# Attention in batches of three units, and attention and scan programs written out without loops

## The chip, the cores and the metric

The kernel runs on one core of a Trainium2 chip. A core has a matrix engine (TensorE, PE in the profile), a vector engine (VectorE, DVE), a scalar engine (ScalarE, ACT), GpSimd (POOL) and SyncE (SP), which issues transfers. Each runs its own program in order, and they meet at semaphores. Matmul results go to PSUM (eight banks of 2 KB per partition); everything else is in SBUF. The metric is the device time of one execution in microseconds.

## The reference, cut to what matters

The input is an image of 48 channels and 128 x 128 pixels. Four layers are applied, each as x = x + f(group_norm(x)). The change touches two of them.

Layer 0 is attention over all 16,384 pixels, one head of 48 channels:

```python
qkv = conv3x3_depthwise(einsum(x, qkv_w)); q, k, v = split(qkv)
q, k = l2norm(q), l2norm(k)
attn = softmax(q @ k.T * temperature)        # 16384 x 16384
out = (attn @ v) @ proj_w.T
```

Layer 2 is a state-space scan over 4,096 tokens of 192 channels, cut here to the rows that matter:

```python
h = exp(d_l[:, None] * A) * h + (d_l * u_l)[:, None] * B_l[None, :]   # 192 x 192 state
y = einsum('dn,n->d', h, C_l)
```

Layer 1 (an 8 x 8 FFT mixing with gates) and layer 3 (integral-image sampling) are not touched.

## The kernel before

**Attention** (`attend`, line 467). The queries are cut into 32 blocks of 512 (`NQB`, `BLK`), and for each block the keys are cut into 64 units (`UNITS`): a unit is 2 x 128 keys against 512 queries, so there are 2,048 units. For each unit:

- PE `score` (line 532): six f16 matmuls, on two halves of 64 rows of the array at a time, into one of two slots of `scores` (two PSUM banks a slot). It waits until ACT has read the slot.
- ACT `exponentials` (line 600): one Exp of 128 x 1024 into one of four slots of `prob` (`RING`).
- DVE `low` (line 633): the difference between the f32 probability and its upper half read as bf16, kept as f16 in `prob_lo`.
- PE `weigh_high` (line 547): four matmuls of the values against the upper halves, on two halves of 64 columns of the array; `weigh_low` (line 559): two matmuls against `prob_lo`. Both add to one of two banks of `sums`. `weigh_low` ends the use of the slot (`used`).

PE's order is written by hand in `pair_of_blocks` (line 574): for every two units it runs `weigh_high` and `weigh_low` of the two units that lie four back (`AHEAD`), then `score` of two new ones. Twice per pair of blocks, `project` (line 568) multiplies the finished sums, which ACT copied to SBUF (`copy_sums`, line 607), with the output weights into the bank `final`; DVE then inverts and multiplies in eight pieces (`invert`, `divide`), spread over the units 16 to 47 of the next block, and POOL adds the block to the image (line 525), once per block.

PE's body is a pair of blocks, written out, and a loop runs it 15 times after a first copy. ACT's and DVE's programs are nested loops: four units are the innermost body, and a block or a pair is the outer one. SP loads a block of queries one block ahead.

**Scan** (`scan`, line 1244). 192 channels are taken in 32 groups of six (`NG`, `GD`). A group has 36 steps (`STEPS`: nine slots of 128 state rows, four chunks of 1,024 tokens). In each step PE spreads delta and delta times u over the partitions (`delta`, `delta_u`: two matmuls each), ACT copies one and takes Exp of the other, POOL multiplies the copy by B (line 1527), and DVE runs one scan of 128 x 1024 (line 1487). Beside this PE computes y of the chunk before (`unit`, `select`), and DVE cuts the diagonal out of it (`extract`, line 1498), four times per nine steps. The state changes between two buffers; in PE's, ACT's, DVE's and POOL's programs the group is the body of a loop. PE and ACT run group 0 as a copy, groups 1 to 30 in the loop and group 31 as a copy; DVE and POOL run groups 1 to 31 in the loop.

Waits whose value comes from a loop register are followed by `nop(nofuse=True)`, an instruction that does nothing; without it the wait can ride on the next instruction.

Of the kernel before, what the change touches and what calls it, by code (L numbers as in the profile page):

```python
# [204 lines left out]
PAIR = 2 * UNITS  # L205
# [4 lines left out]
RING = 4  # L210
PIECES = 8
AHEAD = 4
# [254 lines left out]
def attend(nc, image, halves, values, out_w, bound, temp):  # L467


    with ExitStack() as ctx:  # L470
# [16 lines left out]
        ngroup = UNITS // RING  # L487
        q_hi, q_lo = halves[0, LO, :], halves[1, LO, :]
        k_hi, k_lo = halves[0, HI, :], halves[1, HI, :]
        tops, tails = [slice(r * CHUNK, r * CHUNK + C) for r in range(2)], [slice(r * CHUNK + C, (r + 1) * CHUNK) for r in range(2)]  # L490

# [37 lines left out]
        def _(pe):  # L529
            def score(pair, u, first):  # L530
                slot, g = u // UNITS, u % UNITS
                if g == 0:
                    pe.wait_ge(q_loaded[slot], 128 * (pair + 1))
                if first and slot == 0 and g % (UNITS // KPIECES) == 0:
                    pe.wait_ge(k_loaded[g // (UNITS // KPIECES)], 128)
                if not first or u > 1:
                    pe.wait_ge(prob_ready, pair * PAIR + u - 1)
                pe.nop(nofuse=True)
                for j in range(3):
                    for r in range(2):  # L540
                        part = slice(r * CHUNK, (r + 1) * CHUNK)
                        last = nc.tensor.matmul(scores[:, u % 2, r * BLK:(r + 1) * BLK], keys[part, j, g * KT:(g + 1) * KT],  # L542
                                                queries[part, slot, j, :], start=j == 0, stop=j == 2)
                last.then_inc(scores_ready, 1)

            def weigh_high(pair, u, first=False):
                slot, g = (u // UNITS) % 2, u % UNITS
                if g == 0 and not first:
                    pe.wait_ge(sums_copied, pair * 2 + u // UNITS - 1)
                pe.wait_ge(prob_ready, pair * PAIR + u + 1)  # L550
                pe.nop(nofuse=True)
# [6 lines left out]
            def weigh_low(pair, u):  # L558
                slot, g = (u // UNITS) % 2, u % UNITS
                pe.wait_ge(low_ready, pair * PAIR + u + 1)  # L560
                pe.nop(nofuse=True)
# [5 lines left out]
            def project(b, first=False):  # L567
                pe.wait_ge(sums_copied, b + 1)
                if not first:
                    pe.wait_ge(divided, b * PIECES)  # L570
                pe.nop(nofuse=True)
                nc.tensor.matmul(final[:, :], out_w[:, :], sums_sb[:, :], start=True, stop=True).then_inc(projected, 1)

            def pair_of_blocks(pair, first=False):
                for u in range(0, PAIR, 2):
                    if not first or u >= AHEAD:
                        for v in (u - AHEAD, u - AHEAD + 1):
                            weigh_high(pair, v, first)
                        for v in (u - AHEAD, u - AHEAD + 1):
                            weigh_low(pair, v)  # L580
                    if u == 12 and not first:
                        project(pair * 2 - 1)
                    if u == UNITS + 12:
                        project(pair * 2, first)
                    score(pair, u, first)
                    score(pair, u + 1, first)

            pair_of_blocks(0, first=True)
            with pe.Fori(1, NQB // 2) as pair:
                pair_of_blocks(pair)  # L590
            for u in range(PAIR - AHEAD, PAIR, 2):
                for v in (u, u + 1):
                    weigh_high(NQB // 2 - 1, v)
                for v in (u, u + 1):
                    weigh_low(NQB // 2 - 1, v)
            project(NQB - 1)

        @block.scalar
        def _(act):
            def exponentials(s, j, wait_used=True):  # L600
                act.wait_ge(scores_ready, s + 1)
                if wait_used:
                    act.wait_ge(used, s + 1 - RING)
                nc.scalar.activation(prob[:, j, :], scores[:, j % 2, :], ACT.Exp, bias=bound[:, 0:1],  # L604
                                     scale=temp[:, 0:1]).then_inc(prob_ready, 1)

            def copy_sums(b, slot, first=False):
                act.wait_ge(used, (b + 1) * UNITS)
                if not first:
                    act.wait_ge(projected, b)  # L610
                act.nop(nofuse=True)
                nc.scalar.copy(sums_sb[:, :], sums[:, slot, :]).then_inc(sums_copied, 1)

            def query_block(b, slot, first=False, second=False):
                s0 = b * UNITS
                for j in range(RING):
                    exponentials(s0 + j, j, wait_used=not first)
                for j in range(RING):
                    exponentials(s0 + RING + j, j)
                    if j == 0 and not first:  # L620
                        copy_sums(b - 1, 1 - slot, first=second)
                with act.Fori(2, ngroup) as g:
                    for j in range(RING):
                        exponentials(s0 + g * RING + j, j)
            query_block(0, 0, first=True)
            query_block(1, 1, second=True)
            with act.Fori(1, NQB // 2) as pair:
                for slot in range(2):
                    query_block(pair * 2 + slot, slot)
            copy_sums(NQB - 1, 1)  # L630

        @block.vector
        def _(dve):
            def low(s, j, wait_used=True):
                dve.wait_ge(prob_ready, s + 1)
                if wait_used:
                    dve.wait_ge(used, s + 1 - RING)
                nc.vector.tensor_tensor(prob_lo[:, j, :], prob[:, j, :], prob_hi[:, j, :],  # L638
                                        ALU.subtract).then_inc(low_ready, 1)

            def invert(b, piece, first=False):
                dve.wait_ge(projected, b + 1)
                if not first:
                    dve.wait_ge(added, b)
                dve.nop(nofuse=True)
                q = ds(piece * (BLK // PIECES), BLK // PIECES)
                nc.vector.reciprocal(rden[HI, q], final[LO, q]).then_inc(inverted, 1)

            def divide(b, piece):
                dve.wait_ge(inverted, b * PIECES + piece + 1)  # L650
                dve.nop(nofuse=True)
                q = ds(piece * (BLK // PIECES), BLK // PIECES)
                nc.vector.tensor_tensor(rden[HI, q], final[HI, q], rden[HI, q], ALU.mult).then_inc(divided, 1)  # L653

            def query_block(b, first=False, second=False):
                s0 = b * UNITS
                for j in range(RING):
                    low(s0 + j, j, wait_used=not first)

                def groups(g0, g1, divides=False):  # L660
                    with dve.Fori(g0, g1) as g:
# [14 lines left out]
            with dve.Fori(2, NQB) as b:  # L676
                query_block(b)
# [1499 lines left out]
```

## Time and profile before

| | |
|---|---|
| median of 3 runs | 8340.8 us (8329.88 to 8345.57) |
| the profiled execution | 8343.99 us |
| its span, first to last instruction | 8339.0 us |
| outside the span | 5.0 us |
| PE, DVE, ACT, POOL busy | 80%, 84%, 63%, 40% of the span |
| Exp of attention, first to last start | 426.2 to 3479.6 us |
| first scan step | 4424.6 us |
| Exp in attention (line 604) | 2,048 times, 1202 ns each |
| scans (line 1487) | 1,152 times, 2280 to 2348 ns each |

Busy time of PE is modelled at its end: a matmul is shown with the time in which its result runs out of the array, and the next one starts before that. The distance from one start to the next is what counts. "Issue" behind a wait means that nothing in the profile released the instruction: its engine's sequencer had not handed it over, or the array was not ready. PEclk is the share of the full TensorE clock that was granted.

### The profile page before, as it was taken

How to read it: one execution, taken by the hardware profiler on the slowest of the kernel's cores; microseconds unless marked ns; L12 is line 12 of the kernel's file. 1: busy time of each engine (PE TensorE's matmuls, PEld its weight loads, DVE VectorE, ACT ScalarE, POOL GpSimd, SP SyncE). 2: the span in 40 equal slices, each digit the busy share in tenths (PEclk: the TensorE clock that was granted, in tenths of full speed). 3: DMA queues.
4: the chain of work that ended last, by engine and by line, in shares of the span. 5: the costliest groups of instructions: out<-in, count | busy, mean ns of one | idle time of the engine just before them, and what ended most of it. 6: DMA issues, size and time to landing. Idle time of an engine off the chain costs nothing. (4 is left out here: it accounts for less than half of the span.)

```text
span 8339.0 us, 181301 instructions
## 1 busy us (share of the span) xinstructions
PE 6705.5 (80%) x61152; PEld 2911.9 (35%) x61152; DVE 6983.8 (84%) x6264; ACT 5257.7 (63%) x5277; POOL 3359.4 (40%) x1726
## 2 busy tenths in 40 slices
PE   4999999999999999799697788788878878834321
PEld 2533333333333333255332333333333333322110
DVE  7788888888888888788748999999999999964556
ACT  2177777777777777522187888888888888820000
POOL 1000000000000000000007999999999999934666
PEclk9999999999999999899899999999999999967665
DMA  1020000000000000000020000000000000022222
GB/s 27 26 38 5 5 5 5 7 5 5 5 5 5 7 5 5 4 0 0 12 60 15 6 6 6 6 6 6 6 6 6 6 7 6 6 56 74 67 66 74
DMA packets 116941, 139.45 MB, mean 17 GB/s; under 512 B 49884, under 2 KB 96060, under 8 KB 115148
## 3 DMA queue, kind: packets, MB, share of 16 engines
q1 hardware_dynamic: 91488, 76.06, 3.7%
q0 software_dynamic: 24576, 50.36, 2.3%
q8 instruction: 585, 9.58, 0.5%
q10 hardware_dynamic: 256, 3.15, 0.3%
q14 instruction: 36, 0.29, 0.0%
HBM read 93.83 MB, written 35.65 MB: 16 GB/s over the span
## 5 line engine op out<-in xcount | busy, mean ns | idle before, releaser
L1527 POOL TENSOR_TENSOR k_image<-k_image,s_b 128x1024 f32<-128x1024 f32 x1152 | 2697.0, 2354 | 457.9 <-ACT k_image L1437 421.0
L604 ACT ACTIVATE att_prob<-att_scores,a_bound,a_temp 128x1024 f32<-128x1024 f32 x2048 | 2361.4, 1202 | 692.5 <-PE att_scores L542 689.7
L638 DVE TENSOR_TENSOR att_prob_lo<-att_prob 128x1024 f16<-128x1024 f32 x2048 | 2451.1, 1238 | 410.1 <-ACT att_prob L604 365.7
L542 PE MATMUL att_scores<-att_queries,att_keys 64*128 64x512 f16 x12288 | 1520.6, 380 | 22.7 <-DMA att_keys<-qk_halves 19.2
L1437 ACT COPY k_image<-h_du 128x1024 f32<-128x1024 f32 x1152 | 1169.3, 1015 | 434.4 <-PE h_du L1366 433.2
L525 POOL TENSOR_TENSOR k_image<-k_image,att_rden 48x512 f32 x32 | 69.1, 2159 | 3334.2 <-DVE att_rden L653 3334.2
L1487 DVE TENSOR_TENSOR_SCAN h_state_odd<-h_keep,k_image 128x1024 f32<-128x1024 f32 x576 | 1327.1, 2348 | 0.1
L1444 ACT ACTIVATE h_keep<-h_keep,h_decay 128x1024 f32<-128x1024 f32 x1152 | 1258.8, 1093 | 65.2 <-PE h_keep L1354 44.2
L555 PE MATMUL att_sums<-att_prob,a_values 128*64 128x512 bf16 x8192 | 1136.1, 398 | 42.8 <-issue 42.8
L1354 PE MATMUL h_keep<-h_rows,h_spread 128*128 128x512 bf16 x2304 | 703.0, 387 | 466.2 <-DVE k_image L1487 217.9
L542 PEld LDWEIGHTS att_scores<-att_queries,att_keys 64*128 64x128 f16 x12288 | 540.6, 94 | 928.8 <-issue 627.0
L1366 PE MATMUL h_du<-h_rows,h_spread 128*128 128x512 bf16 x2304 | 714.7, 393 | 126.4 <-issue 98.6
L1487 DVE TENSOR_TENSOR_SCAN k_image<-h_keep,k_image 128x1024 f32<-128x1024 f32 x288 | 648.1, 2280 | 87.4 <-ACT h_keep L1444 79.6
L1487 DVE TENSOR_TENSOR_SCAN k_image<-h_keep,h_state_odd,k_image 128x1024 f32<-128x1024 f32 x288 | 663.5, 2348 | 0.0
L1714 POOL DMA_INDIRECT b_shared<-cells,b_index x512 | 496.0, 969 | 342.9 <-issue 148.6
L563 PE MATMUL att_sums<-att_prob_lo,a_values 128*64 128x512 f16 x4096 | 623.2, 381 | 8.9 <-DVE att_prob_lo L638 8.9
L555 PEld LDWEIGHTS att_sums<-att_prob,a_values 128*64 128x64 f16 x8192 | 372.9, 108 | 715.7 <-issue 483.9
L1354 PEld LDWEIGHTS h_keep<-h_rows,h_spread 128*128 128x128 bf16 x2304 | 157.4, 98 | 997.5 <-issue 988.1
L1764 PE MATMUL b_ps_t<-k_ident,b_mean 128*48 128x128 f32 x128 | 33.5, 417 | 573.3 <-DVE b_mean L1880 373.6
L1797 ACT ACTIVATE b_act<-b_ps_c,b_b,b_back 112x512 f32<-112x512 f32 x32 | 24.9, 777 | 643.4 <-remote 358.1
L563 PEld LDWEIGHTS att_sums<-att_prob_lo,a_values 128*64 128x64 f16 x4096 | 233.1, 110 | 265.0 <-issue 28.5
L1385 PE MATMUL h_y<-h_state_odd,s_c 128*32 128x192 f32 x4096 | 321.2, 350 | 1.8 <-DVE h_state_odd L1487 1.8
(275 smaller groups left out, 7293.3 us busy)
## 6 DMA issues: line engine op xcount, KB each, us to landing
y_rows<-h_y_sb SPq DMA_DIRECT2D x1024, 3.0 KB
att_queries<-qk_halves SPq DMA_DIRECT2D x256, 48.0 KB, 2.0
parts<-t_part SPq DMA_DIRECT2D x48, 192.0 KB, 2.5
h_rows<-parts SPq DMA_DIRECT2D x128, 72.0 KB
b_shared<-cells,b_index POOLq DMA_INDIRECT x512
att_keys<-qk_halves SPq DMA_DIRECT2D x64, 96.0 KB, 7.2
cells<-b_shared SPq DMA_DIRECT2D x4, 1536.0 KB, 5.1
qk_halves<-qkv_hi SPq DMA_DIRECT2D x32, 112.0 KB, 1.8
```

The lines of the kernel that those rows point to most:

```text
L542: last = nc.tensor.matmul(scores[:, u % 2, r * BLK:(r + 1) * BLK], keys[part, j, g * KT:(g + 1) * KT], queries[part, slot, j, :], start=j ...
L555: nc.tensor.matmul(sums[part, slot, :], values[:, r * UNITS + g, part], prob_hi[:, u % RING, r * BLK:(r + 1) * BLK], start=g == 0 and r == ...
L563: last = nc.tensor.matmul(sums[r * CHUNK:(r + 1) * CHUNK, slot, :], values[:, r * UNITS + g, 0:CHUNK], prob_lo[:, u % RING, r * BLK:(r + 1 ...
L604: nc.scalar.activation(prob[:, j, :], scores[:, j % 2, :], ACT.Exp, bias=bound[:, 0:1], scale=temp[:, 0:1]).then_inc(prob_ready, 1)
L638: nc.vector.tensor_tensor(prob_lo[:, j, :], prob[:, j, :], prob_hi[:, j, :], ALU.subtract).then_inc(low_ready, 1)
L1354: last = nc.tensor.matmul(keep[:, k % 2, cols], spread[:, 0, slot, :], rows[:, c % 2, cols], start=True, stop=True)
L1366: last = nc.tensor.matmul(du[:, cols], spread[:, 1, slot, :], rows[:, c % 2, cols], start=True, stop=True)
L1437: nc.scalar.copy(du_sb[k % 3], du[:, :]).then_inc(du_copied, 1)
L1444: nc.scalar.activation(keep[:, k % 2, :], keep[:, k % 2, :], ACT.Exp, scale=decay[:, ds(g * SLOTS + k // STEPS * SLOTS + k % SLOTS, 1)]).t ...
L1487: nc.vector.tensor_tensor_scan(out=state[c % 2][:, slot, :], data0=keep[:, k % 2, :], data1=drive[k % 3], initial=initial, op0=ALU.mult, o ...
L1527: nc.gpsimd.tensor_tensor(drive[k % 3], du_sb[k % 3], b[:, c * CH:(c + 1) * CH], ALU.mult).then_inc(drive_ready, 1)
L1714: nc.gpsimd.indirect_dma_start(got[:, y % GOT, k * CELL:(k + 1) * CELL], None, cells, bass.IndirectOffsetOnAxis(index[:, k, y:y + 1], 0)). ...
```

## The change

- Attention works in batches of three units (`BATCH`): three slots of `scores` (six banks), a ring of six in `prob` and `prob_lo`, and weighing six units back. A batch is `weigh_high` of three, `weigh_low` of three, `score` of three. Batches run on over the ends of blocks.
- The bank `final` goes: `project` writes its result into the bank of `sums` that it was computed from, and the first `weigh_high` of a block waits for `divided` of the block two back instead of for `sums_copied`.
- `project` comes after the weighing of unit 12 of the next block, `copy_sums` after the Exp of unit 6, and `invert` and `divide` run in the units 18 to 49.
- All loops of the two stages on PE, ACT, DVE and POOL are written out, apart from POOL's loop over blocks in attention. SP's loops stay. Waits have constant values, and the `nop(nofuse=True)` are gone.

```diff
+BATCH = 3
-RING = 4
+RING = 2 * BATCH
-AHEAD = 4
+AHEAD = 2 * BATCH
+PROJECT_AT = 12
+INVERT_FROM = 18
...
-        scores = n.ps("scores", [P, 2, 2 * BLK])
+        scores = n.ps("scores", [P, BATCH, 2 * BLK])
-        final = n.ps("final", [SPAN, BLK])
...
+            def score(u):
+                b, g, slot = u // UNITS, u % UNITS, u // UNITS % 2
...
+                wait_past(pe, prob_ready, u + 1 - BATCH)
...
+            def weigh_high(u):
+                if g == 0:
+                    wait_past(pe, divided, (b - 1) * PIECES)
+                pe.wait_ge(prob_ready, u + 1)
...
+            def project(b):
                 pe.wait_ge(sums_copied, b + 1)
+                nc.tensor.matmul(sums[0:SPAN, b % 2, :], out_w[:, :], sums_sb[:, :], start=True, stop=True).then_inc(projected, 1)
+
+            for u0 in range(0, ALL_UNITS + AHEAD, BATCH):
+                weighed = [u for u in range(u0 - AHEAD, u0 - AHEAD + BATCH) if 0 <= u < ALL_UNITS]
+                for u in weighed:
+                    weigh_high(u)
+                for u in weighed:
+                    weigh_low(u)
+                for u in weighed:
+                    if u >= UNITS and u % UNITS == PROJECT_AT:
+                        project(u // UNITS - 1)
+                for u in range(u0, u0 + BATCH):
+                    if u < ALL_UNITS:
+                        score(u)
...
+            for u in range(ALL_UNITS):
+                act.wait_ge(scores_ready, u + 1)
+                wait_past(act, used, u + 1 - RING)
+                nc.scalar.activation(prob[:, u % RING, :], scores[:, u % BATCH, :], ACT.Exp, bias=bound[:, 0:1],
                                      scale=temp[:, 0:1]).then_inc(prob_ready, 1)
+                if u >= UNITS and u % UNITS == RING:
+                    copy_sums(u // UNITS - 1)
...
+            for u in range(ALL_UNITS):
+                low(u)
+                b, g = u // UNITS, u % UNITS
+                if b and g >= INVERT_FROM and g < INVERT_FROM + 4 * PIECES:
+                    piece, step = divmod(g - INVERT_FROM, 4)
+                    if step == 0:
+                        invert(b - 1, piece)
+                    if step == 2:
+                        divide(b - 1, piece)
...
             delta(0, 0)
             delta_u(0, 1)
-            group(0, first=True)
-            with pe.Fori(1, NG - 1) as g:
-                group(g)
-            group(NG - 1, last=True)
+            for g in range(NG):
+                group(g, first=g == 0, last=g == NG - 1)
```

The last edit stands in the same form in ACT's, DVE's and POOL's scan programs.

## Rows read from the trace of the kernel before

**Rows 1.** Two windows (attention, scan): busy us of PE, PEld, DVE, ACT, POOL; clock, DMA.

```profile
424.00:3484.00 3060.00, 3003.28 (x24639) 1155.27 (x24640) 2644.34 (x2544) 2373.22 (x2080) 67.83 (x31) 0.99 0.03 7
4424.00:7324.00 2900.00, 2326.48 (x31018) 1006.64 (x31018) 2807.67 (x1660) 2406.17 (x2556) 2695.16 (x1152) 0.98 0.02 6
```

**Rows 2.** Timeline of attention: start us, length us, engine, line, operation, count [idle before].

```profile
2001.12 1.47 PE L542 MATMUL att_scores<-att_queries,att_keys 64*128 64x512 f16 x12
2002.06 2.30 ACT L604 ACTIVATE att_prob<-att_scores,a_bound,a_temp 128x1024 f32<-128x1024 f32 x2 [0.57 <-PE att_scores L542]
2002.52 1.10 PE L555 MATMUL att_sums<-att_prob,a_values 128*64 128x512 bf16 x8
2003.46 0.60 PE L563 MATMUL att_sums<-att_prob_lo,a_values 128*64 128x512 f16 x4
2003.99 1.25 PE L542 MATMUL att_scores<-att_queries,att_keys 64*128 64x512 f16 x10
```

**Rows 3.** The same timeline from inside two of these runs of matmuls.

```profile
2002.99 0.63 PE L555 MATMUL att_sums<-att_prob,a_values 128*64 128x512 bf16 x4
...
2003.67 0.38 PE L563 MATMUL att_sums<-att_prob_lo,a_values 128*64 128x512 f16 x2
```

**Rows 4.** Timeline of POOL in attention: one addition per query block.

```profile
590.05 2.15 POOL L525 TENSOR_TENSOR k_image<-k_image,att_rden 48x512 f32 x1 [499.33 <-DVE att_rden L653]
683.49 2.17 POOL L525 TENSOR_TENSOR k_image<-k_image,att_rden 48x512 f32 x1 [91.28 <-DVE att_rden L653]
...
873.68 2.19 POOL L525 TENSOR_TENSOR k_image<-k_image,att_rden 48x512 f32 x1 [94.56 <-DVE att_rden L653]
...
3459.49 2.19 POOL L525 TENSOR_TENSOR k_image<-k_image,att_rden 48x512 f32 x1 [91.27 <-DVE att_rden L653]
```

**Rows 5.** Timeline of PE at the end of a pair of blocks.

```profile
989.52 1.86 PE L555 MATMUL att_sums<-att_prob,a_values 128*64 128x512 bf16 x8 [2.85 <-issue]
```

**Rows 6.** Busy time by engine in the stretch behind that.

```profile
989.60:993.00 3.40, 3.40 (x17) 1.24 (x17) 0.24 (x1) 0.00 (x0) 0.00 (x0) 0.50 0.30 81
```

**Rows 7.** Timeline of PE at a projection and at unit 50.

```profile
1010.01 1.11 PE L572 MATMUL att_final<-att_sums_sb,a_out_w 128*112 128x512 f32 x2
1011.06 1.47 PE L542 MATMUL att_scores<-att_queries,att_keys 64*128 64x512 f16 x12
...
1068.49 0.41 PE L563 MATMUL att_sums<-att_prob_lo,a_values 128*64 128x512 f16 x2 [0.27 <-DVE att_prob_lo L638]
```

**Rows 8.** Timeline of DVE while it inverts and divides.

```profile
1033.48 2.36 DVE L638 TENSOR_TENSOR att_prob_lo<-att_prob 128x1024 f16<-128x1024 f32 x2
1035.87 0.23 DVE L653 TENSOR_TENSOR att_rden<-att_final,att_rden  x1
...
1038.63 0.55 DVE L647 RECIPROCAL att_rden<-att_final  x1
1039.21 2.36 DVE L638 TENSOR_TENSOR att_prob_lo<-att_prob 128x1024 f16<-128x1024 f32 x2
```

**Rows 9.** Timeline of DVE at the first steps of scan groups 1, 2 and 31.

```profile
4513.00 4.51 DVE L1487 TENSOR_TENSOR_SCAN k_image<-h_keep,k_image 128x1024 f32<-128x1024 f32 x2
...
4600.62 2.29 DVE L1487 TENSOR_TENSOR_SCAN k_image<-h_keep,k_image 128x1024 f32<-128x1024 f32 x1
4606.07 2.29 DVE L1487 TENSOR_TENSOR_SCAN k_image<-h_keep,k_image 128x1024 f32<-128x1024 f32 x1 [3.16 <-ACT h_keep L1444]
...
7236.50 4.47 DVE L1487 TENSOR_TENSOR_SCAN k_image<-h_keep,k_image 128x1024 f32<-128x1024 f32 x2
```

**Rows 10.** Timeline of PE at the start of scan group 2.

```profile
4602.84 1.01 PE L1366 MATMUL h_du<-h_rows,h_spread 128*128 128x512 bf16 x2 [3.70 <-issue]
```

**Rows 11.** Timeline of PE in the convolution ahead of attention.

```profile
220.69 1.89 PE L191 MATMUL qkv_ps_qk<-qkv_x_split,qkv_qk_split 112*112 x8
222.42 1.02 PE L409 MATMUL qkv_ps_n<-qkv_sq,qkv_ones 112*112 112x512 f32 x2
```

**Rows 12.** The DMA queues in attention: packets, MB, share of 16 engines.

```profile
q8 instruction: 251, 4.11, 0.6%
```

More of the change, by code:

```diff
@@ L204 @@
 UNITS = KHALF // KT
-PAIR = 2 * UNITS
+ALL_UNITS = NQB * UNITS
+BATCH = 3
 CHUNK = 64
@@ L529, in _ @@
         def _(pe):
-            def score(pair, u, first):
-                slot, g = u // UNITS, u % UNITS
+            def score(u):
+                b, g, slot = u // UNITS, u % UNITS, u // UNITS % 2
                 if g == 0:
[L533 to L538, printed above, removed]
+                    pe.wait_ge(q_loaded[slot], 128 * (b // 2 + 1))
+                if b == 0 and g % piece_units == 0:
+                    pe.wait_ge(k_loaded[g // piece_units], 128)
+                wait_past(pe, prob_ready, u + 1 - BATCH)
                 for j in range(3):
@@ L541, in score @@
                         part = slice(r * CHUNK, (r + 1) * CHUNK)
-                        last = nc.tensor.matmul(scores[:, u % 2, r * BLK:(r + 1) * BLK], keys[part, j, g * KT:(g + 1) * KT],
+                        last = nc.tensor.matmul(scores[:, u % BATCH, r * BLK:(r + 1) * BLK], keys[part, j, g * KT:(g + 1) * KT],
                                                 queries[part, slot, j, :], start=j == 0, stop=j == 2)
                 last.then_inc(scores_ready, 1)
[L546 to L551, printed above, removed]
+            def weigh_high(u):
+                b, g, slot = u // UNITS, u % UNITS, u // UNITS % 2
+                if g == 0:
+                    wait_past(pe, divided, (b - 1) * PIECES)
+                pe.wait_ge(prob_ready, u + 1)
                 for r in range(2):
@@ L599, in _ @@
         def _(act):
[L600 to L604, printed above, removed]
-                                     scale=temp[:, 0:1]).then_inc(prob_ready, 1)
[L607 to L630, printed above, removed]
+            def copy_sums(b):
+                act.wait_ge(used, (b + 1) * UNITS)
+                wait_past(act, projected, b)
+                nc.scalar.copy(sums_sb[:, :], sums[:, b % 2, :]).then_inc(sums_copied, 1)
+            for u in range(ALL_UNITS):
+                act.wait_ge(scores_ready, u + 1)
+                wait_past(act, used, u + 1 - RING)
+                nc.scalar.activation(prob[:, u % RING, :], scores[:, u % BATCH, :], ACT.Exp, bias=bound[:, 0:1],
+                                     scale=temp[:, 0:1]).then_inc(prob_ready, 1)
+                if u >= UNITS and u % UNITS == RING:
+                    copy_sums(u // UNITS - 1)
@@ L649, in divide @@
             def divide(b, piece):
                 dve.wait_ge(inverted, b * PIECES + piece + 1)
-                dve.nop(nofuse=True)
                 q = ds(piece * (BLK // PIECES), BLK // PIECES)
[L653 to L661, printed above, removed]
-                        for j in range(RING):
-                            low(s0 + g * RING + j, j)
-                            if divides and j == 1:
-                                invert(b - 1, g - g0, second)
-                        if divides:
-                            divide(b - 1, g - g0)
-                if first:
-                    groups(1, ngroup)
-                else:
-                    groups(1, 4)
-                    groups(4, 4 + PIECES, divides=True)
-                    groups(4 + PIECES, ngroup)
@@ L674, in _ @@
-            query_block(0, first=True)
-            query_block(1, second=True)
-            with dve.Fori(2, NQB) as b:
-                query_block(b)
+                nc.vector.tensor_tensor(rden[HI, q], sums[HI, b % 2, q], rden[HI, q], ALU.mult).then_inc(divided, 1)
+            for u in range(ALL_UNITS):
[7 more added lines that the diff above has]
+                        divide(b - 1, piece)
@@ L1468, in _ @@
             copy_du(0, 1)
-            group(0, first=True)
-            with act.Fori(1, NG - 1) as g:
-                group(g)
-            group(NG - 1, last=True)
+            for g in range(NG):
+                group(g, first=g == 0, last=g == NG - 1)
             for half in range(2):
@@ L1511, in group @@
                     recur(g, k)
-            group(0, first=True)
-            with dve.Fori(1, NG) as g:
-                group(g)
+            for g in range(NG):
+                group(g, first=g == 0)
             for slot in range(SLOTS):
@@ L1524, in group @@
                     wait_past(pool, state_ready, s - 2)
-                    pool.nop(nofuse=True)
                     b = b_c[0 if slot < GD else 1]
@@ L1528, in group @@
                                             ALU.mult).then_inc(drive_ready, 1)
-            group(0)
-            with pool.Fori(1, NG) as g:
+            for g in range(NG):
                 group(g)
```

62 lines of the change are left out of this document (12 added, 50 removed).

## The prediction

> **What bounds the kernel now.** I read the busy time by engine in the two changed stages first. In attention PE is busy 3003 of 3060 us, DVE 2644, ACT 2373; in the scan DVE is busy 2808 of 2900 us, POOL 2695, PE 2326 [rows 1]. So PE should set the pace of attention and DVE that of the scan. The timelines then show what the share can't.
>
> In attention one turn of PE's program takes 2003.99 - 2001.12 = 2.87 us for two units, 1.435 us a unit [rows 2], and PE stands in front of no wait: score, weigh_high, weigh_low and the next score follow each other. But they don't follow at an even pace. Matmuls come in pairs that share the array. The twelve of a score pair of units take 1.47 us from the first start to the last end, and one takes 0.38 us [rows 2, 3], so six pairs start within 1.09 us, 0.218 us apart. From the last of them (2002.21) to the first weigh_high (2002.52) it is 0.31 us. Inside weigh_high the distance is (2003.46 - 2002.99) / 2 = 0.235 us, in weigh_low 2003.67 - 2003.46 = 0.21 us, and from the last weigh_low to the next score 2003.99 - 2003.67 = 0.32 us [rows 2, 3]. So twice per turn, where the array goes from halves of rows to halves of columns and back, some 0.1 us is lost. The turn from weigh_high to weigh_low, which also has waits, loses nothing. ACT is not the limit: it has 0.57 us idle per turn [rows 2].
>
> The timeline of POOL gives the length of each block, as it adds one block each. It has 31 additions. From 590.05 to 683.49 is 93.44 us, but 873.68 comes 2.19 + 94.56 = 96.7 us after the one before, and this longer distance returns at every second block [rows 4]. There PE issues nothing for 2.85 us [rows 5] and then runs at a granted clock of 0.50, which is the 1.2 GHz level, for 3.4 us [rows 6]. It is the point where PE's loop over pairs jumps back. In the scan the same thing stands at each group: group 1, which PE and ACT reach from the copy of group 0 without a jump, takes 4600.62 - 4513.00 = 87.62 us; at the start of group 2 PE issues nothing for 3.70 us [rows 10], and the second scan waits 3.16 us for ACT's Exp [rows 9]. From group 2 to group 31 the 29 groups take 7236.50 - 4600.62 = 2635.88 us, 90.89 each [rows 9]. Group 31 starts with two scans back to back (4.47 us for two), though DVE and POOL jump there as well; PE and ACT don't. So the jumps of DVE and POOL cost nothing that shows.
>
> **The change part by part.** The sum is made against the profiled execution: 8344.0 us, of which 8339.0 are span. The median is 3.2 us less.
>
> *Three units per turn.* A turn now has a third unit: three more score pairs (3 x 0.218 = 0.65), two of weigh_high (2 x 0.235 = 0.47) and one of weigh_low (0.21), 1.33 us, and no further change of the array's halves. Turn: 2.87 + 1.33 = 4.20 us, 1.400 a unit, 0.035 less than now; x 2,048 = 72 us. The bounds: nothing, if what is lost belongs to the unit and not to the turn; 98 us, if every one of the six added pairs comes at 0.215 us (turn 4.16). I take 72, since the distances were read at the very places that multiply.
>
> A page weighs this otherwise. The Trainium skill (TensorEngine Tiling (Array Packing), Key Properties) says that a change of tiling mode drains the engine. With a full drain the next matmul would start when the last is out, 0.38 us after its start, 0.16 more than a pair's distance; two of those are 0.32 us per turn, and the saving would be 0.32 x (1/2 - 1/3) x 2,048 = 109 us. The rows show 0.31 and 0.32 us, so a partial drain.
>
> *Does anything else keep up with 4.20 us?* ACT: two Exps take 2.30 us [rows 2], three 3.45; 0.75 us are free, and copy_sums (about half an Exp's elements, some 0.6 us) fits once per block. The third score needs the third Exp of the turn before. An Exp starts 0.94 us after its score's first matmul (2002.06 - 2001.12), so the three of a turn end at 0.94 + 3.45 = 4.39 us, and the third score of the next turn starts at 4.20 + 1.31 = 5.51: 1.1 us to spare, and copy_sums takes 0.6 of it. The ring of six holds: weigh_low of six units back ends ahead of the score, and the Exp comes later still. DVE: while it inverts and divides, four units take 1039.21 - 1033.48 = 5.73 us, of which 2 x 2.36 + 0.23 + 0.55 = 5.50 are busy [rows 8]. PE will want 5.60. If 5.73 is DVE's own limit, it falls 0.13 us behind in each of eight pieces, 1.0 us per block. DVE finishes the low of a turn's third unit near 0.94 + 3.45 + 1.3 = 5.7 us after the turn's first score, and weigh_low of it comes at about 4.20 + 1.96 + 1.41 + 0.42 = 8.0: 2.3 us of cover. So nothing; 31 x 1.0 = 32 us without that cover.
>
> *project* keeps its price: 1011.06 - 1010.01 = 1.05 us of PE per block [rows 7]. That it writes into `sums` makes the block after next wait for `divided`, which is complete at unit 50 of the next block; that wait is never late.
>
> *The jumps in attention.* 3459.49 - 590.05 = 2869.4 us are 30 blocks; at 93.45 they would be 2803.5. The loop costs 66 us (14 jumps within this, 4.7 us each, idle PE and the low clock behind it together) [rows 4 to 6]. Written out, all of it goes. What is late next is PE itself.
>
> *The inner loops of ACT and DVE.* A straight block has 32 turns (91.8) and project (1.05); 93.45 - 92.85 = 0.6 us are left. One piece is the wait of weigh_low for DVE at unit 50, where DVE goes from one of its loops to the next [rows 7]; another is copy_sums. With straight programs and the deeper ring I take all: 31 x 0.6 = 19 us. Bounds 0 and 19.
>
> *The scan.* 29 x (90.89 - 87.62) = 95 us [rows 9]. DVE is then without a gap, and its pace is measured in group 1 and stays. POOL has 2695 / 1,152 = 2.34 us per step [rows 1] against 87.62 / 36 = 2.43, so it follows, with little to spare. At least the 3.16 us wait of rows 9 less what DVE had in hand goes; I see no reason for a part of it to stay.
>
> *The nops.* Without them a wait can ride on the next instruction. DVE's and ACT's attention instructions had none before. On PE the place to look is the convolution: its second instruction group (line 409) carries its wait without a nop, and starts 222.42 - (220.69 + 1.89 - 0.38) = 0.22 us after the last matmul, the ordinary distance [rows 11]. Nothing either way.
>
> *Filling the programs.* PE's attention is the same number of matmuls, read once. The instruction queue brought 251 blocks in attention, 0.6% of the DMA engines [rows 12], and PE ran through most of them in straight stretches of two blocks without a loss. Nothing for the fetch of longer programs.
>
> Sum: 72 + 66 + 19 + 95 = 252 us. Profiled execution 8092, median 8340.8 - 252 = 8089 us.
>
> **The rivals.**
> *DVE becomes the bound of attention while it divides.* For it: 5.73 us against 5.60. Against it: 5.73 is also exactly twice PE's turn, so DVE may only follow, and there is cover. It gives back 32 us: 8121.
> *The loss belongs to the unit, not to the turn.* Then batches of three bring nothing: 8161. Against it: the loss stands at the two changes of halves alone.
> *The full drain.* By the matmul's own length the two changes would cost 0.32 us per turn: 109 instead of 72 us, 8052. The page named above would have it so; the rows speak for less.
> *Slower: waits on PE's weight loads expose them.* In a turn of three there are nine waits, seven of which are not at a change of halves. If a wait that rides on a weight load keeps it from being loaded under the running matmuls, each costs what a change does, 0.1 us: 7 x 683 turns x 0.1 = 478 us, 8567. It decides from 252 / 4,781 = 0.053 us a wait. For it: each of these loads was ahead of time only because the nop took the wait. Against it: rows 11, though with the whole array and not halves.
> *Slower or less: the fetch of straight programs.* ACT and DVE had short bodies in attention and now run through some 6,000 instructions each, 24 blocks of 256. If each new block stopped the engine as a jump does, 2.85 us, attention would lose 137 us and the scan more, some 70 blocks. It decides from 252 / 118 = 2.1 us a block. Against it: PE meets far more blocks and shows the loss at jumps only. The Trainium skill (Runtime: NRT & Kernel Launch, Instruction fetch mechanics) states just this: fetch ahead is sequential, and a taken branch out of the window stops it; by that rule, too, nothing stays, and the trace agrees with its even 93.45 us.
>
> **How the numbers follow.** Forecast 0.70, DVE bound 0.10, no gain from the turn 0.06, full drain 0.06, weight loads 0.05, fetch 0.03. The forecast's own spread is the 98 against 72 us on one side (8063) and the 19 us of the inner loops on the other (8108). To leave out no more than 2 in 10, the range reaches to the full drain below and the no-gain case above: 8048 to 8165. This program can be told from no change by 0.2%, 17 us. Faster needs one of the first four, or a small price in the last two: 0.92. Within 0.2%: 0.02. Slower: 0.06.
>
> **What would show it.** POOL's additions evenly 4.20 x 64 / 3 + 1.05 = 90.6 us apart, with no longer distance at every second one, shows turns, inner loops and jumps right at once; 92.5 would be the loss in the unit. A turn's timeline should hold 18, 12 and 6 matmuls in 4.20 us. All scan groups should be 87.6 us, and the granted clock 1.00 throughout both stages. PE idle for DVE's low at the units 18 to 49 would be the first rival; weight loads that start with their matmuls inside a run of equal ones, the slower one. Most of all the prediction would be wrong if the stall at PE's jump returned somewhere in the straight program.

## The result

The changed kernel takes 8076.3 us (median of 4 runs, 8070.6 to 8077.7) against 8342.5 us of the kernel before (4 runs beside it). The ratio is 0.9682, 95% interval 0.967 to 0.9695. The forecast was 8089 us, so the gain is 266 us where 252 were expected. The profiled execution's span is 8075.4 us instead of 8339.0.

The busy time by engine in the two stages of the changed kernel, as in [rows 1]:

```profile
425.00:3320.00 2895.00, 2883.49 (x24636) 1180.49 (x24630) 2635.80 (x2563) 2334.74 (x2081) 65.91 (x32) 1.00 0.03 7
4253.00:7056.00 2803.00, 2206.78 (x30510) 976.23 (x31018) 2801.54 (x1660) 2411.65 (x2556) 2698.89 (x1152) 1.00 0.02 6
```

PE in attention and DVE in the scan now have next to no idle time, and the granted clock is 1.00 in both. From the first Exp of attention to the last it is 3304.4 - 425.1 = 2879.3 us (3053.4 before), from the first scan to the last 7053.8 - 4253.5 = 2800.4 us (2897.2 before). These are 174 and 97 us less. Some 7 us were lost elsewhere, in code that wasn't changed: the stretch between attention and scan takes 949.1 instead of 945.0 us, the one behind the scan 1021.5 instead of 1017.2, and what is ahead of attention 1 us less. Why isn't shown. The first of these stretches lies anywhere from 943.7 (low_first) to 951.6 us (two_visits) in the experiments below, none of which touches it.

POOL's timeline in attention, one addition per query block, against [rows 4]:

```profile
585.18 2.06 POOL L527 TENSOR_TENSOR k_image<-k_image,att_rden 48x512 f32 x1 [495.75 <-DVE att_rden L616]
675.28 2.07 POOL L527 TENSOR_TENSOR k_image<-k_image,att_rden 48x512 f32 x1 [88.04 <-DVE att_rden L616]
765.41 2.08 POOL L527 TENSOR_TENSOR k_image<-k_image,att_rden 48x512 f32 x1 [88.07 <-DVE att_rden L616]
855.37 2.10 POOL L527 TENSOR_TENSOR k_image<-k_image,att_rden 48x512 f32 x1 [87.87 <-DVE att_rden L616]
...
3287.35 2.10 POOL L527 TENSOR_TENSOR k_image<-k_image,att_rden 48x512 f32 x1 [87.88 <-DVE att_rden L616]
```

The distances are 90.10, 90.13 and 89.96 us and repeat so to the end, (3287.35 - 585.18) / 30 = 90.07 on the mean. No second block is longer any more. The repeat over three blocks is the turn of three against 64 units.

PE's timeline in attention, against [rows 2, 3, 7]:

```profile
1701.99 2.12 PE L542 MATMUL att_scores<-att_queries,att_keys 64*128 64x512 f16 x18
1704.04 1.55 PE L554 MATMUL att_sums<-att_prob,a_values 128*64 128x512 bf16 x12
1705.42 0.81 PE L561 MATMUL att_sums<-att_prob_lo,a_values 128*64 128x512 f16 x6
1706.16 1.11 PE L567 MATMUL att_sums<-att_sums_sb,a_out_w 128*112 128x512 f32 x2
1707.21 2.12 PE L542 MATMUL att_scores<-att_queries,att_keys 64*128 64x512 f16 x18
```

A turn holds 18, 12 and 6 matmuls and takes 2.05 + 1.38 + 0.74 = 4.17 us (forecast 4.20); the mean of the 451 turns without a projection between 1,200 and 3,200 us is 4.173. The projection still costs 1.05 us. 64 / 3 turns of 4.173 us and 1.05 us are 90.07 us: nothing is left over in a block.

ACT's and DVE's timelines show how much is in hand:

```profile
1693.62 0.59 ACT L588 COPY att_sums_sb<-att_sums 128x512 f32<-128x512 f32 x1
1694.51 3.40 ACT L593 ACTIVATE att_prob<-att_scores,a_bound,a_temp 128x1024 f32<-128x1024 f32 x3 [0.30 <-PE att_scores L542]
1698.68 3.40 ACT L593 ACTIVATE att_prob<-att_scores,a_bound,a_temp 128x1024 f32<-128x1024 f32 x3 [0.78 <-PE att_scores L542]
```

```profile
1029.74 2.36 DVE L604 TENSOR_TENSOR att_prob_lo<-att_prob 128x1024 f16<-128x1024 f32 x2
1032.13 0.55 DVE L611 RECIPROCAL att_rden<-att_sums 48x64 f32<-48x64 f32 x1
1032.71 2.36 DVE L604 TENSOR_TENSOR att_prob_lo<-att_prob 128x1024 f16<-128x1024 f32 x2
1035.11 0.23 DVE L616 TENSOR_TENSOR att_rden<-att_sums,att_rden 48x64 f32<-48x64 f32 x1
1035.37 5.71 DVE L604 TENSOR_TENSOR att_prob_lo<-att_prob 128x1024 f16<-128x1024 f32 x4
```

ACT waits 0.78 us per turn for scores, and the copy of the sums fits into one such wait and leaves 0.30 us. On DVE a low now starts 0.26 us after the start of a divide. In the kernel before it was 1036.24 - 1035.87 = 0.37 us:

```profile
1034.91 2.30 ACT L604 ACTIVATE att_prob<-att_scores,a_bound,a_temp 128x1024 f32<-128x1024 f32 x2 [0.57 <-PE att_scores L542]
1036.24 2.36 DVE L638 TENSOR_TENSOR att_prob_lo<-att_prob 128x1024 f16<-128x1024 f32 x2
```

The first of these Exps, 1.20 us long, ends at 1036.11, and the low that reads it starts 0.13 us later, so it waited for the Exp and not for the divide. DVE had been following ACT there, and ACT in turn PE. DVE's own limit was 5.73 - 0.11 = 5.62 us for four units, about what the rows above show (1035.37 - 1029.74).

In the scan, DVE's timeline at the starts of groups 2 and 31, against [rows 9]:

```profile
4428.09 4.44 DVE L1424 TENSOR_TENSOR_SCAN k_image<-h_keep,k_image 128x1024 f32<-128x1024 f32 x2
...
6968.50 2.26 DVE L1424 TENSOR_TENSOR_SCAN k_image<-h_keep,k_image 128x1024 f32<-128x1024 f32 x1
```

These 29 groups take (6968.50 - 4428.09) / 29 = 87.60 us each, the 87.62 us that group 1 took before.

### The profile page after: what moved, and what is told of

It reads as the page before. It is cut to its first block and busy times, and to the rows that moved or that the text cites. A ratio compares the mean times of both kernels' runs of the same rounds, so it can differ in the third digit from the quotient of the medians.

```text
span 8075.4 us, 153634 instructions
## 1 busy us (share of the span) xinstructions
PE 6464.9 (80%) x60643; PEld 2907.0 (36%) x61152; DVE 6964.3 (86%) x6264; ACT 5223.3 (65%) x5277; POOL 3370.7 (42%) x1726
## 5 line engine op out<-in xcount | busy, mean ns | idle before, releaser
L593 ACT ACTIVATE att_prob<-att_scores,a_bound,a_temp 128x1024 f32<-128x1024 f32 x2048 | 2320.5, 1201 | 558.2 <-PE att_scores L542 558.0
L542 PE MATMUL att_scores<-att_queries,att_keys 64*128 64x512 f16 x12288 | 1447.3, 378 | 19.3 <-DMA att_keys<-qk_halves 19.3
L554 PE MATMUL att_sums<-att_prob,a_values 128*64 128x512 bf16 x8192 | 1056.5, 391 | 0.0
L1313 PE MATMUL h_du<-h_rows,h_spread 128*128 128x512 bf16 x1796 | 585.6, 385 | 105.0 <-issue 80.4
L554 PEld LDWEIGHTS att_sums<-att_prob,a_values 128*64 128x64 f16 x8192 | 400.6, 108 | 602.0 <-issue 288.9
L561 PE MATMUL att_sums<-att_prob_lo,a_values 128*64 128x512 f16 x4096 | 554.1, 378 | 0.0
L1302 PEld LDWEIGHTS h_keep<-h_rows,h_spread 128*128 128x128 bf16 x2304 | 133.1, 97 | 1076.5 <-DVE h_state_odd L1424 489.3
L1331 PE MATMUL h_y<-k_image,s_c 128*32 128x192 f32 x4096 | 324.0, 336 | 0.0
```

The lines of the kernel that those rows point to most:

```text
L542: last = nc.tensor.matmul(scores[:, u % BATCH, r * BLK:(r + 1) * BLK], keys[part, j, g * KT:(g + 1) * KT], queries[part, slot, j, :], star ...
L554: nc.tensor.matmul(sums[part, slot, :], values[:, r * UNITS + g, part], prob_hi[:, u % RING, r * BLK:(r + 1) * BLK], start=g == 0 and r == ...
L561: last = nc.tensor.matmul(sums[r * CHUNK:(r + 1) * CHUNK, slot, :], values[:, r * UNITS + g, 0:CHUNK], prob_lo[:, u % RING, r * BLK:(r + 1 ...
L593: nc.scalar.activation(prob[:, u % RING, :], scores[:, u % BATCH, :], ACT.Exp, bias=bound[:, 0:1], scale=temp[:, 0:1]).then_inc(prob_ready, 1)
L1302: last = nc.tensor.matmul(keep[:, k % 2, cols], spread[:, 0, slot, :], rows[:, c % 2, cols], start=True, stop=True)
L1313: last = nc.tensor.matmul(du[:, cols], spread[:, 1, slot, :], rows[:, c % 2, cols], start=True, stop=True)
```

## The experiments

The expectations give totals as on the chip of the first comparison. The chips of the experiments run the kernel before in 8218 to 8222 us and the changed kernel in 7952 us (after_again, 0.9676): what lies behind the scan takes 894 us there instead of 1021, with attention and scan alike. So the ratios are against the kernel before on the same chip, and the changed kernel is compared by its blocks and groups, whose lengths are the same on both. Where a total is said to lie above the changed kernel's, it is against the 7952.1 us of after_again, beside which only low_first and dense_pieces ran; the others ran on other chips.

**Batches of two, all else straight (b2_straight).**

```diff
-BATCH = 3
+BATCH = 2
```

> The changed kernel with batches of two (two score slots, ring of four, weighing four units back), all programs still without loops. My theory: a turn costs 2.87 us as in the kernel before, and the straight programs of ACT and DVE alone remove the 0.6 us that each block had left over, so POOL's additions stand 32 x 2.87 + 1.05 = 92.9 us apart and the attention stage takes (1.435 - 4.173 / 3) x 2048 = 90 us longer than in the changed kernel: 8166 us. Rival one: the loss belongs to the unit and not to the turn (then the batch brings nothing and this kernel takes 8076 us). Rival two: the 0.6 us went because the ring became deeper; then the blocks stay at 93.45 us and the kernel takes 8185 us.

It takes 8047.0 us, ratio 0.9789 (0.9773 to 0.9805), some 95 us above the changed kernel. POOL's timeline in attention:

```profile
684.20 2.07 POOL L527 TENSOR_TENSOR k_image<-k_image,att_rden 48x512 f32 x1 [90.93 <-DVE att_rden L616]
...
3381.46 2.09 POOL L527 TENSOR_TENSOR k_image<-k_image,att_rden 48x512 f32 x1 [90.93 <-DVE att_rden L616]
```

29 blocks take 2697.26 us, 93.01 each, and none is longer. So batches of three are worth 93.01 - 90.07 = 2.94 us a block. A turn of two takes 2.867 us in the traces of this kernel and of the kernel before, so 32 turns and a projection are 92.79 us. A straight block of the kernel before had 93.45 - 92.79 = 0.66 us left over, of which 0.44 are gone here and 0.22 stay; the turn itself accounts for 2.72 of the 2.94 us. Rival one (loss per unit) falls. Rival two (the ring did it) falls for two thirds of what was left over.

Where the 0.44 us went, the two traces show turn by turn: some 0.37 us near unit 50, where DVE went from one of its loops to the next, and 0.09 at copy_sums. That it was the loops of ACT and DVE alone isn't shown: this kernel also projects into `sums`, inverts and divides one unit later and has no nops.

**PE's loop back in the scan (scan_pe_loop), and its counterpart (scan_others_loop).**

```diff
-            for g in range(NG):
-                group(g, first=g == 0, last=g == NG - 1)
+            group(0, first=True)
+            with pe.Fori(1, NG - 1) as g:
+                group(g)
+            group(NG - 1, last=True)
```

The first has this on PE, with the nops; the second has the old loops and nops on ACT, DVE and POOL.

> The changed kernel with PE's program of the scan as it was before (loop over groups 1 to 30, with its nops); ACT, DVE and POOL stay without loops. My theory: the stall at a group's start is PE's jump alone, so groups take 90.9 us again and the kernel 8076 + 29 x 3.3 = 8172 us, with PE at the clock level 0.50 for a few us at each group. Rival: ACT's jump is as much to blame, as ACT's loop had the same bounds; then this kernel loses only part of it, down to nothing (8076 us) if it was ACT's alone.

> The counterpart: the changed kernel with the scan programs of ACT, DVE and POOL as they were before (loops and nops), PE's without a loop. My theory: jumps of these three cost nothing that shows, so groups take 87.6 us and the kernel 8076 us, within 8. Rival (ACT's jump is to blame): groups of about 90.9 us, 8172 us. If both this kernel and the one with PE's loop are slow, any jump costs.

PE's loop: 8046.0 us, ratio 0.9786 (0.9769 to 0.9802), 94 us slower than the changed kernel, groups of 90.90 us. The others' loops: 7956.1 us, ratio 0.9676 (0.966 to 0.9692), no slower, groups of 87.58 us. DVE's timeline at group 2, first with PE's loop, then with the others':

```profile
4427.57 2.29 DVE L1430 TENSOR_TENSOR_SCAN k_image<-h_keep,k_image 128x1024 f32<-128x1024 f32 x1
4432.95 2.29 DVE L1430 TENSOR_TENSOR_SCAN k_image<-h_keep,k_image 128x1024 f32<-128x1024 f32 x1 [3.09 <-ACT h_keep L1391]
```

```profile
4430.88 4.47 DVE L1430 TENSOR_TENSOR_SCAN k_image<-h_keep,k_image 128x1024 f32<-128x1024 f32 x2
```

PE's timeline at the same place, and its clock in the window behind it, both with PE's loop:

```profile
4429.79 1.01 PE L1315 MATMUL h_du<-h_rows,h_spread 128*128 128x512 bf16 x2 [3.70 <-issue]
```

```profile
4428.20:4434.00 5.80, 3.87 (x30) 1.76 (x32) 2.71 (x2) 2.01 (x2) 2.14 (x2) 0.52 0.08 17
```

DVE names ACT's Exp as what it waited for, and ACT's own loop is straight here. The stall of 3.70 us is that of [rows 10], at the same group. It is PE's alone.

The trace also records the branch itself, at the end of PE's loops (ns, least, median and most of all passes). First the kernel before, its loop over pairs of blocks and its loop over groups, then scan_pe_loop:

```profile
L589 PEldq COMPARE_BRANCH  x15: 76/3578/3898, 795.6 to 3478.2; - x15
L1423 PEldq COMPARE_BRANCH  x30: 83/3527/3851, 4598.7 to 7234.6; - x30
L1372 PEldq COMPARE_BRANCH  x30: 83/3552/3884, 4425.7 to 7061.7; - x30
```

The last pass of each loop, which doesn't jump back, is the one of 76 or 83 ns; the jumps take 3.3 to 3.9 us. In attention they take as long as in the scan.

**How long may PE's body be (pe_loop_short, pe_loop_mid, pe_loop_most).** All three have PE's loop and leave out part of y: the second and third matmul group of each unit, in four, two or one of a group's four chunks.

```diff
-                for stat, d0, d1, s0 in ((2, 0, GD, 0), (3, 0, half_d, GD), (4, half_d, GD, GD)):
+                for stat, d0, d1, s0 in ((2, 0, GD, 0), (3, 0, half_d, GD), (4, half_d, GD, GD))[:3 if c in (0, 2) else 1]:
```

(This is the middle one; the short one has `()`, the long one `(0, 2, 3)`. The nops are back with the loop. Each was run twice.)

> The changed kernel with PE's loop in the scan, and a shorter body: the two smaller of the three matmul groups of each unit are left out in all four chunks (part of y is not computed), so one group has some 1,110 instructions on PE by the profile's count, where the loop before has 2,130. DVE's work is the same. My theory: a jump stalls PE only where the body is longer than what the instruction memory holds, since PE's loops of 380 and 579 instructions in other stages show no gap; so groups take 87.6 us and PE's clock stays at 1.00 at their start. Rival: a jump always costs some 4 us and the other loops hide it behind waits; then groups take about 90.9 us.

> The same with the two smaller matmul groups left out in two chunks of four: some 1,620 instructions in PE's body. If the size decides, this tells on which side of it the limit lies: groups of 87.6 us (it still fits) or of about 90.9 us (it doesn't). By the Trainium skill (Runtime: NRT & Kernel Launch, Instruction fetch mechanics), PE's instruction memory holds 2,048, and it should fit.

> The same with the two smaller matmul groups left out in one chunk of four: some 1,870 instructions in PE's body. It should still fit by 2,048, unless the blocks of 256 at its two ends are counted whole: 1,870 instructions can touch nine blocks, eight are held. So 87.6 us a group, or a stall as with the full body; I hold these for equally likely.

7958.8, 7958.8 and 8044.2 us, ratios 0.9681, 0.9681 and 0.9785. The windows of groups 2 to 30 of the short, middle, long and full body (columns as in [rows 1]; the second count is of weight loads):

```profile
4429.50:6975.70 2546.20, 1760.01 (x13224) 494.92 (x13456) 2542.91 (x1509) 2187.53 (x2321) 2441.60 (x1045) 0.98 0.02 5
```

```profile
4429.30:6976.80 2547.50, 1870.11 (x20503) 698.79 (x20880) 2542.86 (x1509) 2183.63 (x2321) 2442.03 (x1045) 0.99 0.02 5
```

```profile
4428.70:7061.70 2633.00, 1966.05 (x24188) 813.89 (x24594) 2546.32 (x1510) 2183.07 (x2321) 2442.20 (x1045) 0.98 0.02 6
```

```profile
4427.60:7063.60 2636.00, 2034.57 (x27842) 916.80 (x28306) 2545.64 (x1510) 2181.58 (x2321) 2443.72 (x1045) 0.98 0.03 6
```

Over 29 groups that is 464, 720, 848 and 976 weight loads a group, and as many matmuls; with waits and register operations PE's body has 1,098, 1,605, 1,860 and 2,114 recorded instructions. The groups take 87.8, 87.8, 90.8 and 90.9 us. PE's branch in the short, the middle and the long one:

```profile
L1372 PEldq COMPARE_BRANCH  x30: 76/208/218, 4427.6 to 6973.8; - x30
L1372 PEldq COMPARE_BRANCH  x30: 76/208/211, 4427.4 to 6974.9; - x30
L1372 PEldq COMPARE_BRANCH  x30: 82/3511/3961, 4426.8 to 7059.8; - x30
```

It is a step, not a slope: up to 1,605 instructions the jump takes 0.21 us, from 1,860 on 3.3 us and more. The rival (any jump costs, hidden elsewhere) falls, and so does the thought that the shorter bodies hide a stall behind PE's spare time: there is no stall to hide.

One part of the expectation missed. PE's clock doesn't stay at 1.00 in the two shorter ones: it falls to 0.50 for 3.4 us at a time, 23 times between groups 2 and 31 of the short one and 14 times of the middle one, mostly not at a jump. In the changed kernel it never does between these groups. This, not the jump, goes with the 0.2 us that these groups take more: 11 of the 29 groups of the short one and 14 of the middle one take 87.59 us, just as without a loop. PE has less work in these two; that the falls come from this isn't shown.

Why the step comes below 2,048 isn't shown. My guess, that blocks of 256 count whole at both ends, would fit, but I had given the long body even odds.

**Twice the changes of the array (two_visits).**

```diff
+                scored = [u for u in range(u0, u0 + BATCH) if u < ALL_UNITS]
                 for u in weighed:
                     weigh_high(u)
+                for u in scored[:1]:
+                    score(u)
                 for u in weighed:
                     weigh_low(u)
...
-                for u in range(u0, u0 + BATCH):
-                    if u < ALL_UNITS:
-                        score(u)
+                for u in scored[1:]:
+                    score(u)
```

> The changed kernel with the number of changes between halves of rows and halves of columns doubled: a turn is weigh_high of three, score of one, weigh_low of three, score of two, instead of weigh_high, weigh_low, score. Same matmuls. My theory: each change costs 0.1 us over a pair's distance, two more per turn make 4.17 + 0.2 = 4.37 us, and 683 turns 137 us: 8213 us. By a full drain (0.16 us a change) it would be 4.49 us and 8295 us. If the loss belonged to the unit, the turn would stay at 4.17 us and the kernel at 8076 us.

8105.8 us, ratio 0.986 (0.9843 to 0.9876), 154 us above the changed kernel. PE's timeline:

```profile
1700.43 0.82 PE L542 MATMUL att_scores<-att_queries,att_keys 64*128 64x512 f16 x6
1701.19 0.84 PE L561 MATMUL att_sums<-att_prob_lo,a_values 128*64 128x512 f16 x6
1701.96 1.47 PE L542 MATMUL att_scores<-att_queries,att_keys 64*128 64x512 f16 x12
1703.36 1.55 PE L554 MATMUL att_sums<-att_prob,a_values 128*64 128x512 bf16 x12
1704.83 0.82 PE L542 MATMUL att_scores<-att_queries,att_keys 64*128 64x512 f16 x6
```

The turn is 1704.83 - 1700.43 = 4.40 us, 0.23 more: 0.11 us per added change, nearer to my 0.1 than to the full drain's 0.16.

**DVE's load doubled while it divides (dense_pieces).**

```diff
-                if b and g >= INVERT_FROM and g < INVERT_FROM + 4 * PIECES:
-                    piece, step = divmod(g - INVERT_FROM, 4)
+                if b and g >= INVERT_FROM and g < INVERT_FROM + 2 * PIECES:
+                    piece, step = divmod(g - INVERT_FROM, 2)
...
-                    if step == 2:
+                    if step == 1:
```

> The changed kernel with invert and divide of one piece in every two units instead of four (units 18 to 33). It doubles DVE's load in that stretch. My theory of the cover: DVE needs about 3.34 to 3.45 us for two units there, PE 2.78, so DVE falls 4.5 to 5.3 us behind over eight pieces and has 2.3 us of cover: PE waits for low some 2.2 to 3.0 us per block, 68 to 93 us in all. If the cover were none, it would be 140 to 165 us; if DVE had much more in hand than I worked out, nothing.

8046.2 us, ratio 0.9787 (0.9772 to 0.9802), 94 us above the changed kernel, just past my upper number. DVE's timeline, and PE's wait at the end of the stretch:

```profile
1671.61 1.23 DVE L604 TENSOR_TENSOR att_prob_lo<-att_prob 128x1024 f16<-128x1024 f32 x1
1672.87 0.23 DVE L616 TENSOR_TENSOR att_rden<-att_sums,att_rden 48x64 f32<-48x64 f32 x1
...
1674.38 0.55 DVE L611 RECIPROCAL att_rden<-att_sums 48x64 f32<-48x64 f32 x1
1674.96 1.23 DVE L604 TENSOR_TENSOR att_prob_lo<-att_prob 128x1024 f16<-128x1024 f32 x1
```

```profile
1677.76 0.41 PE L561 MATMUL att_sums<-att_prob_lo,a_values 128*64 128x512 f16 x2 [0.51 <-DVE att_prob_lo L604]
```

Two units take DVE 1674.96 - 1671.61 = 3.35 us and PE 2.78, so DVE falls 0.57 us behind per piece, 4.6 us in all, and a block grows by 94 / 31 = 3.0 us. The cover is thus about 1.5 us and not 2.3, an estimate from these two numbers.

**The nops back on PE (nops_back).** `pe.nop(nofuse=True)` again behind the waits of score, weigh_high and weigh_low.

> The changed kernel with the nop behind the waits of score, weigh_high and weigh_low back on PE (6,144 of them, waits on constants). My theory: they cost nothing, the turn stays 4.17 us and the kernel at 0.968 of the kernel before. Rival: part of what the turn came out below my 4.20 us (weigh_high's pairs stand 0.226 instead of 0.235 us apart) is the missing nops; then the turn is about 4.20 us and the kernel 18 us slower.

7952.6 us, ratio 0.9673 (0.9657 to 0.9689), against 7952.1 without. A turn is 4.17 us and a block 90.07 us in both. On PE in attention the nops cost nothing, and a wait without one costs nothing either.

**weigh_low first (low_first), beside the changed kernel again (after_again).** The two loops of a turn change places, the start flag moves to weigh_low, `used` to weigh_high, and the ring is seven.

```diff
-RING = 2 * BATCH
+RING = 2 * BATCH + 1
-AHEAD = 2 * BATCH
+AHEAD = 2 * BATCH + 1
...
                 for u in weighed:
-                    weigh_high(u)
+                    weigh_low(u)
                 for u in weighed:
-                    weigh_low(u)
+                    weigh_high(u)
```

> The changed kernel once more, unedited, beside the two others of this call: blocks of 90.07 us, scan groups of 87.59 us, 0.968 of the kernel before. It gives their difference its footing, since the chips of the later calls run the kernel before in another time (8221 us) than the first.

> The changed kernel with weigh_low ahead of weigh_high in each turn, and a ring and distance of seven units instead of six. My theory: the first weigh_high pair behind a change of halves takes 0.25 us, the first f16 pair behind one 0.23 us; with weigh_low first the turn is 0.02 us shorter, 14 us in all (0.2%), if DVE's low is there in time. Rival: the 0.25 us belongs to the first bf16 pair wherever it stands, and nothing is gained; or DVE is late while it divides, since weigh_low now comes 1.4 us earlier, and blocks grow.

7952.1 us (7949.4 to 7955.0) for the changed kernel and 7947.2 us (7944.7 to 7948.3) for the reordered one, five runs each, ratios 0.9676 and 0.9667. PE's timeline of the reordered kernel:

```profile
1703.94 0.84 PE L563 MATMUL att_sums<-att_prob_lo,a_values 128*64 128x512 f16 x6
1704.61 1.52 PE L552 MATMUL att_sums<-att_prob,a_values 128*64 128x512 bf16 x12
1706.07 2.12 PE L542 MATMUL att_scores<-att_queries,att_keys 64*128 64x512 f16 x18
1708.12 0.84 PE L563 MATMUL att_sums<-att_prob_lo,a_values 128*64 128x512 f16 x6
```

The turn is 1708.12 - 1703.94 = 4.18 us, 4.173 on the mean, as in the changed kernel; attention takes 2878.9 us in both traces. DVE wasn't late, but there was nothing to gain in the turn. The reordered kernel is 5 us faster (0.06%), by run times that don't overlap, and not in attention: its trace is 5 us shorter between attention and scan and 3 us longer behind, in code that is the same. I have no version that is faster by its turn.

## Why the prediction was right

*Jumps, attention: 66 us.* The blocks of b2_straight, with batches of two as in the kernel before but straight programs, are even, and in the kernel before PE's 14 jumps take 3.4 to 3.9 us each, as long as those of the scan, where scan_pe_loop shows them to be the cause. The rest of the 4.7 us would be the low clock behind each, which no run separates. Attention's own jump was not put back by itself, so that all of the 66 us are PE's rests on this likeness.

*Jumps, scan: 95 us.* Measured 97 from the first scan to the last, and 94 us come back with PE's loop alone. Two readings carried it: group 1, reached without a jump, as the price of a group without the stall, and group 31, where DVE and POOL jump and nothing is lost.

*Three units per turn: 72 us.* Here the size was off. A unit takes 2.867 / 2 - 4.173 / 3 = 0.0425 us less, 87 us over 2,048 units. The term that was mis-sized is the price of the third unit: 1.33 us, where 4.173 - 2.867 = 1.31 is measured. By its parts the score came out as forecast (2.046 - 1.399 = 0.65), and so did weigh_low (0.744 - 0.529 = 0.21); weigh_high took 1.383 - 0.938 = 0.44 us more and not 0.47. The forecast had read 0.235 us for one of its pairs from two distances with starts to the hundredth of a us; to the thousandth they are 0.233 and 0.228 (medians), and in a run of six pairs all distances behind the first are 0.226. What looks like 0.02 us is 15 us over 683 turns.

*Inner loops: 19 us.* All that was left over went, 0.66 us a block by the traces, 20 us over 31 blocks. 0.44 of it was gone in b2_straight already, where loops, nops and the place of the pieces changed at once; the other 0.22 us went with batches of three and their deeper ring. (POOL adds 32 blocks, the last at 3492.76 us and out of step; the forecast counted 31.)

*DVE's cover: nothing lost.* Right, with less to spare than I worked out: about 1.5 us instead of 2.3. But the need was smaller too, as 5.73 us was PE's pace. DVE's limit of 5.62 us stands against 4.173 x 4 / 3 = 5.56 for PE, 0.06 us behind per piece, 0.5 us in all.

*Nops and the fetch of straight programs: nothing.* nops_back shows the first for attention. In the scan the nops were back with the loops, and where no jump stalled the groups kept 87.6 us. The second is shown by blocks of 89.95 to 90.14 us and groups of 87.59 to 87.75 us, even to 0.2 us through thousands of instructions.

*The rivals.* The full drain and the loss per unit are told apart by two_visits (0.11 us per change) and b2_straight. The full drain would have given a turn's saving of 109 us where 87 were measured. The slower cases didn't come: no stall returned in a straight program, and the nops made no difference to the turn, so no weight load was held up for want of them.

The sum came out 14 us short: the turn gave 15 us more than forecast, scan and inner loops some 3 more, and 7 were lost in the unchanged stages. That these 7 hid part of the error is luck.

## What to carry to other kernels

Here a loop on TensorE was dear where its body had 1,860 recorded instructions or more, and cheap up to 1,605: look for "issue" of some 3 to 4 us on PE at each pass, with the clock at 0.50 behind it, or for the length of the branch itself, before writing anything out. The engine that names the wait (DVE waiting for ACT's Exp) may be two steps from the one that jumped. In PE-bound code count the changes between row halves and column halves, and let each stretch between them be as long as PSUM allows; take the price of added work from many distances inside a stretch, as 0.01 us too much in one distance, taken twice a turn, is 14 us over 683 turns.

## What the hardware showed that I had not expected

The step in the cost of a jump lies between 1,605 and 1,860 recorded instructions in PE's body: 0.21 us for the jump below, 3.3 to 4.0 us above. The Trainium skill (Runtime: NRT & Kernel Launch, Instruction fetch mechanics) gives PE's memory as 2,048; here a body of 1,860 already stalls in full, so a loop's body has to be shorter than that. The same section lets a taken branch stall when its target is outside a window of two pages, and the prediction drew on this; read for PE, it would have made the bodies of 1,098 and 1,605 stall as well, which they don't. That the memory is what sets the step isn't shown by any run. Bodies of ACT, DVE and POOL in the scan (222, 174 and 112 recorded instructions a group) jump at no visible cost. And a change between halves costs 0.09 to 0.11 us over the ordinary distance of some 0.22 us, less than waiting for the last result (0.38 us after its start) would.
